# Clearing the experts' slots in sixteen pieces during batch 0 instead of eight beside the weight loads

## The chip, the cores and the metric

The kernel runs on one core of one Trainium2 chip. The metric is the device time of one execution in microseconds. Before the change it is 3038.3 us, the median of three runs (3036.37, 3038.3 and 3043.93). A fourth execution was taken with the hardware profiler on; it lasted 3023.01 us, and all rows below are from it.

## What is computed

Two layers, each cross attention and a mixture of experts, on 32 sequences of 256 tokens with 256 features:

```python
x = x + L0_xattn(layernorm(x), ctx, ctx, Wq..bo)          # 16 heads, with projections
x = x + L0_ffn(layernorm(x), P_w, U1, U2, U3, W1, W2, b2) # 12 dense experts in each of two mixtures, top 3
x = x + L1_xattn(layernorm(x), ctx, ctx)                  # 16 heads, no projections
x = x + L1_ffn(layernorm(x), router_w, w_gate, w_up, w_down, ws_gate_up, ws_down)

def L0_ffn(x, ...):
    h = gelu(sum_e C1[:, e] * (x @ W1[e].T))              # "mixture" 1
    return sum_e C2[:, e] * (h @ W2[e].T) + C3 @ b2       # "mixture" 2

def L1_ffn(x, ...):                                       # 8192 tokens, 64 experts, top 8
    pos = cumsum(onehot)[...] - 1;  valid = pos < 128     # each expert has 128 slots
    x_buf = zeros((64 * 128 + 1, 256)).at[where(valid, e * 128 + pos, 64 * 128)].set(x[tok])
    y = silu(x_buf @ w_gate) * (x_buf @ w_up) @ w_down
    return segment_sum(y[slot] * w, tok) + shared_expert(x)
```

The `zeros` of `x_buf` is what the change concerns: a slot that no token takes must hold something harmless, since each expert reads all of its 128 slots at the end.

## The kernel before

**The five queues.** The kernel is written as five programs, one for each engine (`sync_program` at L342, `gpsimd_program` at L474, and those of ScalarE, VectorE and TensorE). All of them walk the same list `order`, made by `pieces()` at L77, and each picks the steps that concern it. A step has a place, a number in units of which 40 are one batch: batch b's steps stand at 40 b plus their entry in `PLACES`, `MIX`, `HALF_PLACES` or `SCATTER`. So the tables set the order on every engine, and the engines wait for each other by semaphores only. An engine works strictly in its order.

**SyncE** (SP in the rows) issues all the plain transfers, each engine instruction going into one hardware queue. It stops where a transfer has to wait for data or for a free buffer, and everything behind it in the list stops too.

**The start.** `sync_program` first loads constants and three chunks of attention weights. Then the list starts. The 12 steps `w_mix`, at the places `W_MIX` (1, 3, 5, 11, 13, 15, 21, ... 35), load the two mixtures' weights in 12 chunks of 128x1024 floats, 512 KB each. They go through two stage buffers in turn (`x_mem` and `router_mem` in the rows); ScalarE (L573, `w_h`) and VectorE (L731, `w_l`) split each chunk in a rounded part and the rest, and a chunk's load waits until the one before the last is split (`v_w`). On VectorE and ScalarE these splits stand in the same order as the first batch's attention work.

**Clearing.** The slots lie in HBM (`expert_slots`, 64 experts x 128 slots, each row 321 floats). Right behind each of the first eight chunk loads, `sync_program` issues one transfer (L425) that writes one 321-float row, `empty_rows`, which lies in SBUF, to the 128 slots of eight experts: 128x8x321 floats, 1284 KB. Behind the eighth follow two transfers of 128 KB that clear spare rows of the output (L430). The same SBUF memory, `row_mem`, later takes batch 0's routed rows, so VectorE's write to it (L789 with `row_mem` as output) waits for `c_init`, and so does the scatter on GpSimd.

**Attention.** Each batch goes through attention twice, A in layer 0 and C in layer 1, each in two halves of eight heads. The halves are numbered u = 0, 1, 2, ... in the order of the list. For a half, SyncE reads keys and queries back from HBM (`spread`: two transfers L404 into `kst`, then two L407 into `qst`, which wait until the stores of the query parts `q_parts`, L356, have landed). Then TensorE has four score steps `s1` (L1117, into `first`), each reduced to row maxima by VectorE (L822, `nm`) before the next may overwrite the bank. The maxima are turned, brought into `qst` by four small transfers (L415, `mT`), and four `s2` steps (L1135) make the scores that ScalarE exponentiates (L653). Buffers of three halves are there, so a spread is issued when the half three before has passed its last `s2`.

**The rest of a batch** is the mixtures: 24 products (L1215) spread through the whole period, so that TensorE has work beside the attention of other batches. After the last batch the 64 experts run.

Of the kernel before, what the change touches and what calls it, by code (L numbers as in the profile page):

```python
# [15 lines left out]
P = 128  # L16
EPS = 1e-5
SENTINEL = -1.0e30
TAKEN = -3.0e30
EMPTIED = 8  # L20


class Queue:
# [48 lines left out]
}  # L72
SCATTER = tuple(158.5 + 2.5 * i for i in range(16))
W_MIX = tuple(10 * s + 1 + 2 * k for s in range(4) for k in range(3))


def pieces(NB, L, NE):  # L77


    halves = sorted((SUBS * b + HALF[kind][h], kind, b, h) for kind in "AC" for b in range(NB) for h in range(2))  # L80
    number = {u[1:]: i for i, u in enumerate(halves)}
    J = {}
    for _, kind, b, h in halves:
        J.setdefault((kind, b), len(J))
    placed = [(p, ("w_mix", i)) for i, p in enumerate(W_MIX)]
    for b in range(NB):
        for what, p in PLACES.items():
            piece = (what[:3], what[3], b) if what[:2] == "ln" else (what, b)
            placed.append((SUBS * b + p, piece))
        placed += [(SUBS * b + p, ("mix", b, n, e)) for n in range(2) for e, p in enumerate(MIX[n])]  # L90
        placed += [(SUBS * b + p, ("scatter", b, i)) for i, p in enumerate(SCATTER)]
        for kind in "AC":
            for h in range(2):
                job = (kind, b, J[kind, b], h, number[kind, b, h])
                for what, table in HALF_PLACES.items():
                    at = table[kind, h]
                    for i, p in enumerate(at):
                        placed.append((SUBS * b + HALF[kind][h] + p, (what, *job, i) if len(at) > 1 else (what, *job)))
    placed.sort(key=lambda v: v[0])
    yield from (piece for _, piece in placed)  # L100
    for e in range(NE + 2):
        if e < NE:
            yield ("e_turn", e)
        if e < NE and e % 2:
            yield ("e_same", e // 2)
        if 0 <= e - 1 < NE:
            yield ("e_gate", e - 1)
        if e >= 2:
            yield ("e_down", e - 2)


def build(nc, x_in, ctx_in, ctxT_in, wqT_in, wkvT_in, woT_in, qk_cols_in, bv_cols_in, bo_in, pw_in, uT_in,
# [28 lines left out]
    with ctx:  # L141
# [200 lines left out]
        def sync_program(sp):  # L342
# [15 lines left out]

            for c in range(FIRST):
                load_chunk(c)  # L360
            emptied = 0
            slots = slots_dram.rearrange("(e c) f -> c e f", c=CAP)
            for what, *a in order:
                if what == "load_x":
# [7 lines left out]
                elif what == "load_ctx":  # L372
                    b, = a
                    sp.wait_ge(p_c, b)
                    sp.wait_ge(p_v, min(NB, max(0, b - 3)))
                    sp.e.dma_start(ctxT[:, :, :], ctxT_in[b].rearrange("(a p) s -> p a s", p=P)).then_inc(c_ctxT, 16)
                elif what == "load_v":
                    b, = a
                    sp.wait_ge(p_c, min(NB, b + 4))
                    sp.wait_ge(p_v, b)  # L380
                    sp.e.dma_start(ctx_tok[:, :, :], ctx_in[b].rearrange("(t p) d -> p t d", p=P)).then_inc(c_ctx, 16)
                elif what == "ctx_split":
                    b, = a
                    sp.wait_ge(a_c, b + 1)
                    sp.wait_ge(p_c, b + 1)
                    store_parts(k_dram[1, b], ctx_parts, KEY_PARTS, c_kc)
                elif what == "store_K":
                    b, = a
                    sp.wait_ge(v_k, 2 * (b + 1))
                    store_parts(k_dram[0, b], k_nat, KEY_PARTS, c_k)  # L390
                elif what in ("store_A", "store_C"):
                    b, = a
                    J = job_J[what[-1], b]
                    sp.wait_ge(v_q, q_parts_of(J))
                    store_parts(q_dram[J], q_nat, QUERY_PARTS, c_q)
                elif what == "spread":
                    layer, b, J, h, u = a
                    done, ks = (c_k, k_dram[0, b]) if layer == "A" else (c_kc, k_dram[1, b])
                    sp.wait_ge(done, 48 * (b + 1))
                    if u >= 3:  # L400
                        sp.wait_ge(t_s2, 4 * (u - 2))
                    sp.wait_ge(p_const, 2)
                    for k in range(2):
                        sp.e.dma_start(row_block(k_st[u % 3], k, 0, K1), heads_of(ks, h, k)).then_inc(c_spread[u % 3], 16)  # L404
                    sp.wait_ge(c_q, 48 * (J + 1))
                    for k in range(2):
                        sp.e.dma_start(row_block(q_st[u % 3], k, 0, K1), heads_of(q_dram[J], h, k)).then_inc(  # L407
                            c_spread[u % 3], 16)
                elif what == "max_rows":
                    kind, b, J, h, u = a  # L410
                    sp.wait_ge(a_mT, u + 1)
                    for part in range(2):
                        for k in range(2):
                            r0 = (part * 2 + k) * HP
                            sp.e.dma_start(row_block(q_st[u % 3], k, K1 + part, 1),  # L415
                                           mT[u % 2][r0:r0 + HP, :].bitcast(F32)).then_inc(c_m[u % 2], 16)
                elif what == "d_down":
                    b, = a
                    sp.wait_ge(v_xd, b + 1)
                    sp.e.dma_start(out_rows(b), X[b % NXB][:, :, :]).then_inc(c_out[b % 2], 16)  # L420
                elif what == "w_mix":
                    load_chunk(FIRST + a[0])
                    if emptied < NE:
                        sp.wait_ge(p_const, 1)
                        sp.e.dma_start(slots[:, emptied:emptied + EMPTIED, :],  # L425
                                       empty_rows.unsqueeze(1).broadcast_to([P, EMPTIED, ROW])).then_inc(c_init, 16)
                        emptied += EMPTIED
                        if emptied >= NE:
                            for i in range(2):
                                sp.e.dma_start(out_pad[T + i * P:T + (i + 1) * P, :], empty_rows[:, 0:D]).then_inc(c_init, 16)  # L430
                elif what == "e_turn":
                    e, = a
                    if e == 0:
                        sp.wait_ge(t_av, 2 * HALVES)
                        sp.wait_ge(v_w, CHUNKS)

                        def load_expert(n):
                            sp.e.dma_start(ewgu[n], wgu_in[n]).then_inc(c_gu[n], 16)
                            sp.e.dma_start(down_mem[n], wd_in[n]).then_inc(c_down[n], 16)

                        for n in range(3):
                            load_expert(n)
                        sp.wait_ge(v_co, HALVES)
                        sp.wait_ge(p_xc, NB)
                        sp.wait_ge(a_out, HALVES)
                        sp.wait_ge(t_out, HALVES)
                        for s_ in c_scat:
                            sp.wait_ge(s_, 128 * NB)
                        for n in range(NX):
                            sp.e.dma_start(erow[n], slots_dram[n * CAP:(n + 1) * CAP, :]).then_inc(c_er[n], 16)  # L450
                            if n == 2:
                                for s_ in c_out:
                                    sp.wait_ge(s_, 16 * (NB // 2))
                                load_expert(3)
                                load_expert(4)
                elif what == "e_gate":
                    e = a[0] + NW
                    if e < NE:
                        sp.wait_ge(t_eg, e - NW + 1)
                        sp.e.dma_start(ewgu[e % NW], wgu_in[e]).then_inc(c_gu[e % NW], 16)  # L460
                elif what == "e_down":
                    e = a[0] + NW
                    if e < NE:
                        sp.wait_ge(t_ed, e - NW + 1)
                        sp.e.dma_start(down_mem[e % NW], wd_in[e]).then_inc(c_down[e % NW], 16)
                    e = a[0] + NX
                    if e < NE:
                        sp.wait_ge(v_ey, e - NX + 1)
                        sp.wait_ge(v_id, 2 * ((e - NX) // 2 + 1))
                        sp.e.dma_start(erow[e % NX], slots_dram[e * CAP:(e + 1) * CAP, :]).then_inc(c_er[e % NX], 16)  # L470
# [926 lines left out]
```

## Time and profile before

| | before |
|---|---|
| median of three runs | 3038.3 us |
| the profiled execution | 3023.01 us, its span 3021.2 us |
| TensorE busy | 2738.9 us, 91% |
| VectorE busy | 2202.1 us, 73% |
| ScalarE busy | 1039.7 us, 34% |
| GpSimd busy | 820.5 us, 27% |
| the hardware queue that SyncE feeds | 304.20 MB, 35.6% of 16 DMA engines' span |

TensorE is busy nine tenths of nearly every fortieth of the span; the first two fortieths (a slice is 75.5 us) and the experts at the end are the exceptions. In the span's first two slices the DMA engines are busier than in the steady part, and TensorE's granted clock is at its lower level for most of them. In the rows, PEclk is the granted clock as a share of 2.4 GHz, where 0.50 is the level of 1.2 GHz. A time in brackets at the end of a row is how long the engine stood idle before it, and who released it.

### The profile page before, as it was taken

The numbers are of one execution on the slowest core, as the hardware profiler recorded it, in microseconds if no ns is written. First come the engines' busy times: TensorE is split into PE (matmuls) and PEld (weight loads), VectorE is DVE, ScalarE is ACT, GpSimd is POOL, SyncE is SP. The second block draws the span as 40 slices with busy tenths as digits, with TensorE's granted clock in tenths as the row PEclk, the third lists the DMA queues.
The fourth block names the chain that finished last, engine by engine and source line by source line (L and its number), as shares of the span: only waits on it lengthen the run. The fifth ranks groups of instructions, "written<-read, shape, count | busy, mean of one in ns | idle before, by whom it ended". The sixth has DMA issues, their size and how long they took to land. (4 is left out here: it accounts for less than half of the span.)

```text
span 3021.2 us, 61482 instructions
## 1 busy us (share of the span) xinstructions
PE 2738.9 (91%) x23816; PEld 2297.6 (76%) x23816; DVE 2202.1 (73%) x5944; ACT 1039.7 (34%) x1524; POOL 820.5 (27%) x858
## 2 busy tenths in 40 slices
PE   2599999999999999999999999999999999956886
PEld 1388888888888888888888888888888888736775
DVE  2467888887888887888888888888888888733332
ACT  1223433333334333333333333333333333211111
POOL 1000122222222222222222222222222222334334
PEclk7599999999999999999999999999999999967998
DMA  6633444443333333333333333333333331117785
GB/s 196 183 87 97 114 124 111 116 116 110 108 96 89 100 100 100 94 86 94 100 95 94 100 89 100 98 89 83 97 99 100 99 90 43 40 39 211 207 213 126
DMA packets 321183, 327.31 MB, mean 108 GB/s; under 512 B 45405, under 2 KB 302231, under 8 KB 320892
## 3 DMA queue, kind: packets, MB, share of 16 engines
q1 hardware_dynamic: 287100, 304.20, 35.6%
q0 software_dynamic: 33792, 19.17, 3.6%
q8 instruction: 189, 3.10, 0.4%
q14 instruction: 102, 0.84, 0.1%
HBM read 182.18 MB, written 212.37 MB: 131 GB/s over the span
## 5 line engine op out<-in xcount | busy, mean ns | idle before, releaser
L653 ACT ACTIVATE exps<-second 128x1024 f32<-128x1024 f32 x512 | 525.9, 1027 | 785.0 <-PE second L1135 777.1
L548 POOL DMA_INDIRECT expert_slots<-row_mem,sidx x512 | 509.1, 994 | 790.9 <-PE first L1117 553.8
L1215 PE MATMUL mixp<-w_h,r_part_h 128*128 128x256 f32 x3072 | 668.5, 299 | 40.1 <-DVE hid L906 24.0
L822 DVE TENSOR_REDUCE nm<-first 128x4 f32<-128x1024 f32 x512 | 623.2, 1217 | 93.1 <-PE first L1117 93.0
L1215 PE MATMUL mixp<-w_h,r_part_l 128*128 128x256 f32 x3072 | 609.7, 280 | 0.0
L1215 PE MATMUL mixp<-w_l,r_part_h 128*128 128x256 f32 x3072 | 609.3, 279 | 0.0
L1215 PEld LDWEIGHTS mixp<-w_h,r_part_h 128*128 128x128 f32 x3072 | 467.4, 189 | 97.0 <-DVE hid L906 31.7
L1215 PEld LDWEIGHTS mixp<-w_l,r_part_h 128*128 128x128 f32 x3072 | 468.4, 188 | 0.0
L1215 PEld LDWEIGHTS mixp<-w_h,r_part_l 128*128 128x128 f32 x3072 | 468.1, 188 | 0.0
L906 DVE SCALAR_TENSOR_TENSOR x_mem<-mixp,C,x_mem 128x256 f32<-128x256 f32 x768 | 329.6, 477 | 114.6 <-PE mixp L1215 114.2
L906 DVE SCALAR_TENSOR_TENSOR hid<-mixp,C,hid 128x256 f32<-128x256 f32 x704 | 300.7, 474 | 35.8 <-PE mixp L1215 33.8
L1117 PE MATMUL first<-kst,qst 48*128 48x256 f32 x2048 | 248.6, 322 | 61.6 <-DVE nm L822 32.1
L517 POOL TENSOR_TENSOR norm<-norm,minus_half 128x2 f32<-128x2 f32 x128 | 92.3, 721 | 732.6 <-DVE norm L767 731.7
L1151 PE MATMUL attn_out<-exps,vx 128*17 128x256 f32 x4096 | 268.6, 390 | 3.6 <-ACT exps L653 3.4
L1135 PE MATMUL second<-qst,kst 50*128 50x256 f32 x2048 | 239.8, 313 | 16.0 <-ACT exps L653 9.3
L1117 PEld LDWEIGHTS first<-kst,qst 48*128 48x128 f32 x2048 | 159.1, 191 | 117.1 <-DVE nm L822 45.1
L1135 PEld LDWEIGHTS second<-qst,kst 50*128 50x128 f32 x2048 | 158.3, 189 | 70.2 <-issue 35.6
L1151 PEld LDWEIGHTS attn_out<-exps,vx 128*17 128x17 f32 x4096 | 98.4, 98 | 110.6 <-ACT exps L653 23.3
L561 POOL DMA_INDIRECT out<-x_mem,sidx x64 | 99.2, 1550 | 177.4 <-DVE sidx L997 127.6
L659 ACT COPY out_sb<-attn_out 128x512 f32<-128x512 f32 x128 | 74.6, 583 | 176.7 <-PE misc L1162 121.1
L588 ACT ACTIVATE nat_h<-misc,qk_cols 128x256 fp32r<-128x256 f32 x128 | 53.8, 472 | 168.8 <-PE misc L1094 168.8
L762 DVE BATCH_NORM_STATS2 norm<-x_mem 128x6 f32<-128x256 f32 x256 | 95.6, 415 | 4.1 <-POOL x_mem L531 2.8
(211 smaller groups left out, 3687.0 us busy)
## 6 DMA issues: line engine op xcount, KB each, us to landing
kst<-k_parts SPq DMA_DIRECT2D x256, 192.0 KB, 3.8
qst<-q_parts SPq DMA_DIRECT2D x256, 192.0 KB, 4.1
q_parts<-nat_h SPq DMA_DIRECT2D x128, 256.0 KB
k_parts<-ctx_part_h SPq DMA_DIRECT2D x64, 256.0 KB, 2.4
k_parts<-nat_h SPq DMA_DIRECT2D x64, 256.0 KB, 2.4
q_parts<-nat_l SPq DMA_DIRECT2D x64, 256.0 KB
exps<-in_wgu SPq DMA_DIRECT2D x39, 384.0 KB, 4.4
expert_slots<-row_mem SPq DMA_DIRECT2D x8, 1284.0 KB, 12.5
```

The costliest lines, as they stand in the source:

```text
L517: pool.e.tensor_tensor(rstd[kind][:, :], veps[kind][:, :], minus_half[:, :], ALU.pow).then_inc(p_pow[kind], 1)
L548: pool.e.indirect_dma_start(out=slots_dram, out_offset=bass.IndirectOffsetOnAxis(ap=sidx[b % 2][:, t, k:k + 1], axis=0), in_=row[b % 2][:, ...
L561: pool.e.indirect_dma_start(out=out_pad, out_offset=bass.IndirectOffsetOnAxis(ap=eid[e % NID], axis=0), in_=ey[e % NY], in_offset=None, bo ...
L653: act.e.activation(exps[:, j % NU, :, :, :].rearrange("p k t s -> p (k t s)"), second[:, :, :].rearrange("p k s -> p (k s)"), ACT.Exp, sca ...
L659: act.e.copy(out_sb[:, :, :].rearrange("p g s -> p (g s)"), attn_out[:, :]).then_inc(a_out, 1)
L762: dve.e.bn_stats(st[:, t, :], src[:, t, :]).then_inc(*seq.up())
L822: dve.e.tensor_reduce(nm[u % 2][:, :, 2 * j:2 * j + 2].rearrange("p t k -> p k t"), first[:, :, :].rearrange("p k (t s) -> p k t s", t=TIL ...
L906: dve.e.scalar_tensor_tensor(acc, src, c, acc, ALU.mult, ALU.add).then_inc(v_mix, 1)
L1117: m = pe.e.matmul(bank1[k][:, t * S:(t + 1) * S], q_st[u % 3][at, j, t * P:(t + 1) * P], k_st[u % 3][at, j, :], start=True, stop=True)
L1135: m = pe.e.matmul(bank2[k][:, s * S:(s + 1) * S], k_st[u % 3][at, j, s * P:(s + 1) * P], q_st[u % 3][at, j, :], start=True, stop=True)
L1151: m = pe.e.matmul(attn_out[r0:r0 + HD + 1, q * S:(q + 1) * S], vx[:, s, h * H // 2 + HQ * q + i, :], exps[:, (2 * q + i // 2) % NU, i % 2, ...
L1215: m = pe.e.matmul(mixp[q % 2][:, t * D:(t + 1) * D], src[i][:, dt, t * P:(t + 1) * P], wmix[n][j][:, l, dt, :], start=(k == 0), stop=(k == ...
```

## The change

`EMPTIED` becomes 4, so a clearing transfer covers four experts (128x4x321 floats, 642 KB) and there are 16. They no longer follow the chunk loads but are steps of their own, `empty`, at the places 68, 71.5, ... 120.5 of the list, which in batch 0's terms is from the end of its first mixture until after its layer-1 attention has begun. The two transfers for the output's spare rows follow the last.

```diff
-EMPTIED = 8
+EMPTIED = 4
+EMPTY = tuple(68 + 3.5 * i for i in range(16))
-    placed = [(p, ("w_mix", i)) for i, p in enumerate(W_MIX)]
+    placed = [(p, ("w_mix", i)) for i, p in enumerate(W_MIX)] + [(p, ("empty", i)) for i, p in enumerate(EMPTY)]
-            emptied = 0
                 elif what == "w_mix":
                     load_chunk(FIRST + a[0])
-                    if emptied < NE:
-                        sp.wait_ge(p_const, 1)
-                        sp.e.dma_start(slots[:, emptied:emptied + EMPTIED, :],
-                                       empty_rows.unsqueeze(1).broadcast_to([P, EMPTIED, ROW])).then_inc(c_init, 16)
-                        emptied += EMPTIED
-                        if emptied >= NE:
-                            for i in range(2):
-                                sp.e.dma_start(out_pad[T + i * P:T + (i + 1) * P, :], empty_rows[:, 0:D]).then_inc(c_init, 16)
+                elif what == "empty":
+                    n = a[0] * EMPTIED
+                    sp.wait_ge(p_const, 1)
+                    sp.e.dma_start(slots[:, n:n + EMPTIED, :],
+                                   empty_rows.unsqueeze(1).broadcast_to([P, EMPTIED, ROW])).then_inc(c_init, 16)
+                    if n + EMPTIED == NE:
+                        for i in range(2):
+                            sp.e.dma_start(out_pad[T + i * P:T + (i + 1) * P, :], empty_rows[:, 0:D]).then_inc(c_init, 16)
```

The waits on `c_init` are written with `NE // EMPTIED + 2` and so rise from 10 transfers to 18. The instructions of TensorE, VectorE, ScalarE and GpSimd stand in the same order as before; only SyncE's list moves. One line is added ahead of the programs, so most line numbers rise by one.

The first place is SyncE's list at the start, from the spread of half 0 on. Before, a clearing transfer stands behind each chunk (`in_w1T`):

```order
L376 DMA ctxT<-in_ctxT 128x2x256
L352 DMA x_mem<-in_w1T 128x1024 [waits dve_w]
L425 DMA expert_slots<-row_mem 128x8x321
L352 DMA router_mem<-in_w1T 128x1024 [waits dve_w]
L425 DMA expert_slots<-row_mem 128x8x321
L404 DMA kst1<-k_parts 48x4x256 x2
L407 DMA qst1<-q_parts 48x4x256 x2
L370 DMA x_mem<-in_x 128x2x256
```

And now:

```order
L376 DMA ctxT<-in_ctxT 128x2x256
L353 DMA x_mem<-in_w1T 128x1024 [waits dve_w]
L353 DMA router_mem<-in_w1T 128x1024 [waits dve_w]
L404 DMA kst1<-k_parts 48x4x256 x2
L407 DMA qst1<-q_parts 48x4x256 x2
L370 DMA x_mem<-in_x 128x2x256
```

The clearing transfers between the chunks and ahead of the spread of half 1 are gone.

The second place is SyncE's list at the end of the clearing, around the row maxima of half 6 (`qst0<-mT`) and the spread of half 8 (`kst2`, `qst2`). Before:

```order
L415 DMA qst0<-mT 1x4x256 x3
L381 DMA ctxT<-in_ctx 128x2x256
L356 DMA q_parts<-nat_h 128x2x256 [waits dve_q]
L356 DMA q_parts<-nat_l 128x2x256
L356 DMA q_parts<-nat_h 128x2x256
L404 DMA kst2<-k_parts 48x4x256 [waits pe_s2,k_parts_out]
L404 DMA kst2<-k_parts 48x4x256
L407 DMA qst2<-q_parts 48x4x256 [waits q_parts_out]
L407 DMA qst2<-q_parts 48x4x256
```

And now:

```order
L415 DMA qst0<-mT 1x4x256 x3
L381 DMA ctxT<-in_ctx 128x2x256
L426 DMA expert_slots<-row_mem 128x4x321
L357 DMA q_parts<-nat_h 128x2x256 [waits dve_q]
L357 DMA q_parts<-nat_l 128x2x256
L357 DMA q_parts<-nat_h 128x2x256
L426 DMA expert_slots<-row_mem 128x4x321 x3
L430 DMA out<-row_mem 128x256 x2
L404 DMA kst2<-k_parts 48x4x256 [waits pe_s2,k_parts_out]
L404 DMA kst2<-k_parts 48x4x256
L407 DMA qst2<-q_parts 48x4x256 [waits q_parts_out]
L407 DMA qst2<-q_parts 48x4x256
```

One piece now stands ahead of the stores of the query parts, and three with both spare-row transfers stand between those and the spread that TensorE needs next. Of the other twelve pieces, two stand ahead of the query parts for half 4 and two ahead of its spread, three around the spread of half 5, two ahead of the query parts for half 6 and one behind its spread, one behind the key parts before the maxima of half 5, and one between those maxima and the spread of half 7.

## Rows read from the trace of the kernel before

**Rows 1.** The page: TensorE's granted clock in 40 slices of the span

```profile
PEclk7599999999999999999999999999999999967998
```

**Rows 2.** Busy time by stretch: PE, PEld, DVE, ACT, POOL, clock, DMA share, GB/s

```profile
30.00:60.00 30.00, 3.06 (x16) 2.01 (x16) 8.14 (x8) 3.60 (x5) 0.00 (x0) 0.56 0.99 272
...
120.00:146.00 26.00, 15.97 (x70) 12.98 (x70) 15.68 (x45) 3.63 (x5) 0.69 (x1) 0.55 0.35 75
...
180.00:300.00 120.00, 114.37 (x1012) 98.54 (x1013) 93.34 (x234) 37.06 (x53) 7.90 (x9) 0.96 0.34 91
```

**Rows 3.** Timeline, first 90 us, TensorE and ScalarE: start us, duration us, engine, line

```profile
46.32 0.80 PE L1117 MATMUL first<-kst,qst 48*128 48x256 f32 x4 [16.73 <-DMA qst<-q_parts]
...
53.71 1.04 ACT L573 CAST w_h<-router_mem 128x1024 fp32r<-128x1024 f32 x1 [4.78 <-DMA router_mem<-in_w1T]
...
57.20 0.80 PE L1117 MATMUL first<-kst,qst 48*128 48x256 f32 x4 [7.98 <-DVE nm L822]
...
60.16 1.23 DVE L822 TENSOR_REDUCE nm<-first 128x4 f32<-128x1024 f32 x1 [0.89 <-PE first L1117]
...
62.38 0.80 PE L1117 MATMUL first<-kst,qst 48*128 48x256 f32 x4 [2.26 <-DMA qst<-q_parts]
...
79.75 1.02 ACT L653 ACTIVATE exps<-second 128x1024 f32<-128x1024 f32 x1
...
84.15 1.04 ACT L573 CAST w_h<-x_mem 128x1024 fp32r<-128x1024 f32 x1 [3.39 <-DMA x_mem<-in_w1T]
...
87.64 0.80 PE L1117 MATMUL first<-kst,qst 48*128 48x256 f32 x4 [12.58 <-DVE nm L822]
```

**Rows 4.** SyncE's queue in the same stretch, start and duration of issues

```profile
36.43 2.07 SPq L407 DMA_DIRECT2D qst<-q_parts  x2
...
40.15 3.07 SPq L352 DMA_DIRECT2D router_mem<-in_w1T  x1
...
75.34 0.67 SPq L352 DMA_DIRECT2D x_mem<-in_w1T  x1
```

**Rows 5.** Transfers by line over the span: KB each, median us from issue to landing

```profile
qst<-q_parts SPq DMA_DIRECT2D x256, 192.0 KB, 4.1
...
expert_slots<-row_mem SPq DMA_DIRECT2D x8, 1284.0 KB, 12.5
...
x_mem<-in_w1T SPq DMA_DIRECT2D x3, 512.0 KB, 8.8
router_mem<-in_w2T SPq DMA_DIRECT2D x3, 512.0 KB, 4.2
x_mem<-in_w2T SPq DMA_DIRECT2D x3, 512.0 KB, 4.9
```

**Rows 6.** SyncE's queue in batch 0's mixtures: spreads of halves 4, 6, 7 and 8

```profile
176.77 0.79 SPq L407 DMA_DIRECT2D qst<-q_parts  x2
...
224.54 0.79 SPq L407 DMA_DIRECT2D qst<-q_parts  x2
...
241.14 0.93 SPq L407 DMA_DIRECT2D qst<-q_parts  x2
...
250.27 0.44 SPq L381 DMA_DIRECT2D ctxT<-in_ctx  x1
...
256.20 0.79 SPq L407 DMA_DIRECT2D qst<-q_parts  x2
```

**Rows 7.** TensorE at the first s1 of halves 4, 6, 7 and 8

```profile
192.92 0.51 PE L1117 MATMUL first<-kst,qst 48*128 48x256 f32 x4
...
233.56 0.40 PE L1117 MATMUL first<-kst,qst 48*128 48x256 f32 x4
...
247.42 0.40 PE L1117 MATMUL first<-kst,qst 48*128 48x256 f32 x4
...
263.91 0.40 PE L1117 MATMUL first<-kst,qst 48*128 48x256 f32 x4
```

**Rows 8.** VectorE's first write over the cleared row's memory, which waits for the clearing

```profile
303.90 0.73 DVE L789 TENSOR_SCALAR row_mem<-x_mem,norm 128x256 f32<-128x256 f32 x2
```

## The prediction

> **What bounds the kernel now.** I read the page first, for TensorE's clock by slices, then busy times by stretch, then the timeline of the first 90 us on TensorE and ScalarE, and last SyncE's queue and the transfers' times to landing, at the start and again where the clearing goes. In the steady part TensorE is the bound: from 180 to 300 us it is busy 114.4 of 120 us while the DMA engines are busy 34% of the time [rows 2]. At the start it is the reverse. From 30 to 60 us TensorE is busy 3.06 of 30 us, the DMA engines 99%, at 272 GB/s [rows 2]. Those 30 us move some 8.2 MB, and four clearing transfers of 1284 KB, 5.3 MB, are issued in them, so about two thirds of the traffic is clearing that nothing needs before VectorE's write at 303.90 [rows 8]. The reader is to see in [rows 3] that the start is a chain of waits for transfers: the first score product at 46.32 waited 16.73 us for its queries, the split of a weight chunk at 53.71 waited for its load, the score product at 57.20 waited for VectorE, which had that chunk's other half to make first, the one at 62.38 waited for queries again, and the split at 84.15 waited for a load. So there are two questions: how much of the start comes back, and what 16 pieces cost in the steady part, where TensorE has no time to spare.
>
> **The price of a piece.** A chunk of 512 KB into `x_mem` lands in 4.9 us where no clearing is about (`in_w2T`) and in 8.8 us at the median where one stands just ahead of it (`in_w1T`) [rows 5]. The difference, 3.9 us for 1284 KB, is 329 KB/us, and a piece of 642 KB is 1.95 us of the queue.
>
> **What is removed at the start.** First, the chunk that SyncE issues at 40.15 [rows 4] is split from 53.71 on [rows 3], 13.6 us later. Without clearing it lands in 4.2 to 4.9 us [rows 5], at 44.4 to 45.1. SyncE is there no later than now, since the load waits only for the chunk split before it. I take 9.0 us off; the score product at 57.20 follows this split on VectorE by a fixed 3.5 us and goes with it. The wait ahead of the product at 46.32 is then off the path: its queries, last issued before 38.5 [rows 4], land by 42.6 with the median 4.1 us [rows 5], and the product behind it still waits for that chunk on VectorE. Second, the product at 62.38 waited for queries; the reduction that frees its bank ended at 60.16 + 1.23 = 61.39 [rows 3], so 0.9 us more. Third, the chunk issued at 75.34 [rows 4] would land at 80.2 instead of 84.15, but ScalarE is in an exponential until 79.75 + 1.02 = 80.8 [rows 3]: 3.4 us more, and the product at 87.64 follows. Together 9.0 + 0.9 + 3.4 = 13.3 us off. Behind 90 us the chunk loads already land in 4.2 and 4.9 us, and what is late there is the chain of ScalarE, VectorE and TensorE itself, at 1.2 GHz.
>
> The ends for this term: if the first chunk lands in 8.8 us as those behind a clearing do, because the spreads crowd it just as well, its part is 13.6 - 8.8 = 4.8 us and the rest small, so 5 us. At the other end, from 120 to 146 us TensorE is busy 16.0 of 26 us at a mean clock of 0.55 [rows 2]; a denser start may lift the clock earlier, and if half of that work ran at 2.4 GHz it would save 4 us, for 17. I take 13.3, as each of its three pieces has a row.
>
> **What is added in the steady part.** The eight more issues cost SyncE about 0.45 us each (its other issues are of that length), which it has. No engine waits for the pieces but at 303.90 [rows 8], and the last is issued at about 256, 40 us before. So the price is in what is queued behind them, and on each spread I compare the landing of its queries with TensorE's first use. All times here are those of before; the whole pattern moves forward together.
>
> Half 6: two pieces stand ahead of its query parts. The second of its query loads leaves at about 225.0 and lands 4.1 us later, at 229.1; two pieces make it 233.0, and TensorE comes at 233.56 [rows 6, 7]. Cost nothing, with 0.6 us to spare. Half 4 has four pieces ahead, 7.8 us, on a landing at 181.3 and a use at 192.92 [rows 6, 7]: nothing, and half 5's spread is issued right behind for the four products that follow. Half 7: one piece stands ahead of the spread. Second load at 241.6, landing at 245.7; with 1.95 and 0.45 for the issue 248.1, against 247.42 [rows 6, 7]: 0.7 us late. Half 8: one piece ahead of the query parts, three and the two spare-row transfers behind them. From 250.27 [rows 6] the queue takes 256 KB of context, the piece, 768 KB of query parts, three pieces, 256 KB of spare rows and 768 KB of spread, 4616 KB in all; at 329 KB/us that ends at 264.3. The median landing of 4.1 us [rows 5] has 2.3 us of its own spread's 768 KB in it, so 1.8 us remain for the way there and back: 266.1, against TensorE's 263.91 [rows 7]. That is 2.2 us late. The 0.7 of half 7 is contained in it, since SyncE reaches this stretch through the maxima of half 6, which TensorE turns before it gets to half 7. The maxima themselves (L415) stand behind pieces that were issued some 4 us before; I put them at nothing. The ends: nothing at all, if the pieces run faster than 329 KB/us; and, if half 8's queries, issued at 256.20 and landing by 260.8, come later by all four pieces and the spare rows (8.6 us), 269.4, or 5.5 us. I take 2.2, from the count of bytes.
>
> **The sum.** 13.3 off and 2.2 on is 11.1 us off. Against the profiled execution of 3023.0 us (its span is 3021.2) that is 3011.9. The median of the three runs stands 15.3 us above the profiled execution, which I take as the level of the runs and not as part of the change: 3038.3 - 11.1 = 3027.2 us, or 0.37% faster. What a measurement of this kernel can tell from no change is about 0.3%, 9.1 us.
>
> **The rivals.** (1) The start gives back less. The chunk loads are two buffers deep and their splits are interleaved with the score reductions, so a chunk that lands early meets a ScalarE or VectorE that is not free. For it: 8.14 of VectorE's first 30 us are work in a fixed order [rows 2]. Against: both engines' wait rows name the transfer. With 8 off and 2 on, 3032. (2) The clock rises earlier and stays: 4 us more off, 3023. For it the denser start, against it the page, where the second slice is at 0.5 [rows 1] although TensorE is busy over half of the time from 120 to 146. (3) Each piece pays a fixed time in the queue of its own. A 512 KB load lands in 4.2 us [rows 5], of which its bytes at 329 KB/us are 1.6; if the other 2.6 held the queue too, the four pieces ahead of half 8's spread would add 10.4 us, and the sum would be 13.3 off and 12.6 on: 3037.6. Against: four transfers of a spread, 768 KB, land 4.1 us after the last issue, so fixed times overlap.
>
> The Trainium skill, "DMA: Bandwidth & Descriptors", sections "Bandwidth" and "Rules for kernel authors", speaks against the change in this way: it advises at least 1 MiB per DMA and gives a fixed cost of about 2 us each. By that rule eight more transfers would be an estimated 16 us more of the queue if nothing overlapped, and the sum would come out 5 us slower where all of it met TensorE; rival 3 is what it would do at the place where it matters.
>
> (4) Slower. The pieces stand ahead of what TensorE needs next in every half, not only in half 8: the maxima and spreads all land late, and each piece is lost in full. That is 16 x 1.95 = 31.2 on and 13.3 off, 17.9 slower, 3056. It begins to lose where seven of the sixteen pieces are on the path (7 x 1.95 = 13.7). For it: margins of 0.6 us at half 6 and below nothing at 7 and 8. Against: pieces ahead of a wait of SyncE's are through before what they delay is issued, and a late half absorbs the lateness of the one behind it. That the change does not do what it says is excluded by SyncE's list, where no clearing stands before half 3's maxima.
>
> **How the numbers follow.** The forecast, between 9.1 and 14 us off, has 0.50. Rival 2 has 0.12, rival 1 0.20, rival 3 0.09, rival 4 0.09. So faster by over 0.3% is 0.50 + 0.12 = 0.62, within 0.3% is 0.20 + 0.09 = 0.29, slower 0.09. The range runs from 3020, where the start gives 17 and the pieces cost nothing (3021.3), to 3038, where rival 3 is; it leaves out rival 4 and some of the tails.
>
> **What would show it.** In the new profile: the first score product near 41 instead of 46.32, the one at 57.20 near 48, the one at 87.64 near 74; DMA share from 30 to 60 well under 0.99. Then, between 165 and 260, DMA share up from 0.34, with TensorE waiting for `qst<-q_parts` once or twice, 1 to 3 us in all. The prediction is wrong if waits for `qst` or `kst` add up to over 6 us there, if maxima (`qst<-mT`) show as releasers, or if the product at 87.64 moves by under 9 us.

## The result and the profile after

The changed kernel takes 3027.58 us, the median of twelve runs (3020.72 to 3035.74), against 3036.38 us for the kernel before in the same comparison (twelve runs, 3033.5 to 3046.68). The recorded ratio is 0.9966, 95% interval 0.9953 to 0.9978: some 10 us faster, 0.34%. (A recorded ratio is not the quotient of the two medians, which is 0.9971 here; in this study the two differ by up to 0.0008.) It was compared twice more in the course of the experiments and gave 0.9967 (0.9955 to 0.9979) and 0.9971 (0.9959 to 0.9983).

The profiled execution lasted 3025.41 us, 2.4 us more than the profiled one of before. A single execution does not show this gain at its end. Landmarks show why: the gelu near 400 us and the one near 2602 us are 2203.1 us apart in the profile of before, and 2206.1 to 2218.8 us in the 13 others of this study, whose lists are the same in that stretch on all engines; the changed kernel's own three have 2207.0, 2209.6 and 2210.3. So I read each trace up to the gelu near 400 us and leave the time to the repeated runs.

The page of the changed kernel, TensorE's clock in 40 slices, and busy times by stretch with the columns of [rows 2] (the line numbers of SyncE's instructions are one higher than before, those of the other engines' rows shown here are unchanged):

```profile
PEclk9699999999999999999999999999999999957998
...
30.00:60.00 30.00, 6.84 (x32) 5.14 (x32) 10.69 (x11) 5.46 (x7) 0.00 (x0) 1.00 0.69 166
...
120.00:146.00 26.00, 20.54 (x138) 18.09 (x139) 18.45 (x52) 4.28 (x7) 1.97 (x2) 0.74 0.09 32
146.00:180.00 34.00, 30.38 (x269) 24.68 (x268) 16.27 (x43) 14.36 (x20) 0.69 (x1) 0.95 0.73 204
180.00:300.00 120.00, 113.02 (x955) 96.40 (x954) 93.62 (x241) 34.74 (x50) 9.28 (x11) 0.93 0.50 143
```

From 30 to 60 us the DMA share falls from 0.99 to 0.69 and TensorE's busy time doubles; from 180 to 300 us the share rises from 0.34 to 0.50, and TensorE loses a little. The clock of 0.74 from 120 to 146 us, 0.55 before, is no faster start: the steady part, which follows half 2's copy, has moved into that stretch. The 26 us that correspond to it, 12.4 us earlier, look as before:

```profile
107.60:133.60 26.00, 15.97 (x70) 12.98 (x70) 15.59 (x45) 3.66 (x5) 0.69 (x1) 0.54 0.36 76
```

The timeline of the start, to be held against [rows 3]:

```profile
42.88 0.80 PE L1117 MATMUL first<-kst,qst 48*128 48x256 f32 x4 [12.96 <-DMA qst<-q_parts]
...
46.92 1.04 ACT L573 CAST w_h<-router_mem 128x1024 fp32r<-128x1024 f32 x1 [1.25 <-DMA router_mem<-in_w1T]
...
50.41 0.80 PE L1117 MATMUL first<-kst,qst 48*128 48x256 f32 x4 [4.62 <-DVE nm L822]
...
54.65 0.80 PE L1117 MATMUL first<-kst,qst 48*128 48x256 f32 x4 [1.33 <-DVE nm L822]
...
73.04 1.03 ACT L573 CAST w_h<-x_mem 128x1024 fp32r<-128x1024 f32 x1
...
76.52 0.80 PE L1117 MATMUL first<-kst,qst 48*128 48x256 f32 x4 [9.27 <-DVE nm L822]
```

The product at 57.20 is at 50.41, 6.8 us earlier; that at 62.38 at 54.65, 7.7 earlier, its wait for queries gone; that at 87.64 at 76.52, 11.1 earlier. The split at 73.04 waits for no transfer any more.

And TensorE in batch 0's mixtures, against [rows 7], where `attn_out` is the product behind the one that waits:

```profile
235.83 0.57 PE L1117 MATMUL first<-kst,qst 48*128 48x256 f32 x4 [0.76 <-DMA qst<-q_parts]
...
238.79 3.61 PE L1151 MATMUL attn_out<-exps,vx 128*17 128x256 f32 x32
...
256.49 0.72 PE L1117 MATMUL first<-kst,qst 48*128 48x256 f32 x4 [2.59 <-DMA qst<-q_parts]
257.14 3.31 PE L1151 MATMUL attn_out<-exps,vx 128*17 128x256 f32 x32
```

Two waits for queries, at halves 7 and 8. Behind each, 32 products take 3.61 and 3.31 us. In the kernel before they take 2.01; the first of its rows here is a score product between half 7's first one and those 32, which waits 1.68 us for ScalarE:

```profile
250.16 0.50 PE L1135 MATMUL second<-qst,kst 50*128 50x256 f32 x4 [1.68 <-ACT exps L653]
...
250.83 2.01 PE L1151 MATMUL attn_out<-exps,vx 128*17 128x256 f32 x32
...
264.24 2.01 PE L1151 MATMUL attn_out<-exps,vx 128*17 128x256 f32 x32
```

**The two measures used below** are ScalarE's copies of turned maxima (L647). Of half 2, at the end of the start: 146.44 us before, 134.06 after. And the distance from half 6's copy to half 7's, which holds both waits and the low clock between and behind them:

```profile
146.44 0.36 ACT L647 CAST mT<-misc 16x256 fp32r<-16x256 f32 x1 [0.47 <-PE misc L1125]
...
247.41 0.36 ACT L647 CAST mT<-misc 16x256 fp32r<-16x256 f32 x1
266.93 0.36 ACT L647 CAST mT<-misc 16x256 fp32r<-16x256 f32 x1
```

```profile
134.06 0.36 ACT L647 CAST mT<-misc 16x256 fp32r<-16x256 f32 x1 [0.38 <-PE misc L1125]
...
234.89 0.36 ACT L647 CAST mT<-misc 16x256 fp32r<-16x256 f32 x1
261.14 0.36 ACT L647 CAST mT<-misc 16x256 fp32r<-16x256 f32 x1
```

The first fence is before, the second after: 12.4 us won at the start, and a distance of 26.25 instead of 19.52 us, 6.7 us lost. ScalarE's gelu (L667) at 399.16 us before is at 393.46, 5.7 ahead, which is the difference.

### The profile page after: what moved, and what is told of

It is laid out like the page before. It is cut to its first block and busy times, and to the rows that moved or that the text cites. A ratio compares the mean times of both kernels' runs of the same rounds, so it can differ in the third digit from the quotient of the medians.

```text
span 3023.6 us, 61490 instructions
## 1 busy us (share of the span) xinstructions
PE 2752.8 (91%) x23816; PEld 2301.2 (76%) x23816; DVE 2205.9 (73%) x5944; ACT 1040.3 (34%) x1524; POOL 819.7 (27%) x858
```

## The experiments

Two questions: is the gain all from the start and the loss all from the pieces ahead of halves 7 and 8, and what sets the size of each? All fourteen profiled executions, of eleven kernels, in one table (after, after_again and after_third are one kernel, five_behind and five_again another); "gelu" is the one at 399.16 us before.

| kernel | copy of half 2 | distance 6 to 7 | gelu | ratio (95%) |
|---|---|---|---|---|
| before | 146.44 | 19.52 | 399.16 | 1 |
| after | 134.06 | 26.25 | 393.46 | 0.9966 (0.9953 to 0.9978) |
| after_again | 134.62 | 26.23 | 396.36 | 0.9967 (0.9955 to 0.9979) |
| after_third | 133.36 | 25.61 | 394.95 | 0.9971 (0.9959 to 0.9983) |
| gaps | 132.51 | 19.51 | 387.31 | 0.9955 (0.9937 to 0.9972) |
| five_behind | 133.58 | 19.52 | 386.20 | 0.9948 (0.9929 to 0.9967) |
| five_again | 133.01 | 19.54 | 386.59 | 0.9956 (0.9939 to 0.9974) |
| both | 148.73 | 25.66 | 407.63 | 1.0014 (1.0001 to 1.0027) |
| one_behind | 134.51 | 25.96 | 394.61 | 0.9983 (0.9966 to 0.9999) |
| four_behind | 133.62 | 22.19 | 391.30 | 0.9952 (0.9937 to 0.9968) |
| first4_late | 138.10 | 19.52 | 393.01 | 0.9969 (0.9956 to 0.9982) |
| last4_late | 145.02 | 19.53 | 400.07 | 0.9982 (0.9969 to 0.9996) |
| small_early | 149.48 | 19.51 | 403.05 | 0.9999 (0.9981 to 1.0018) |
| big_late | 133.95 | 24.37 | 391.44 | 0.9959 (0.9946 to 0.9972) |

**gaps: all pieces where SyncE's queue is empty.**

```diff
-EMPTY = tuple(68 + 3.5 * i for i in range(16))
+EMPTY = tuple(47.1 + 0.01 * i for i in range(8)) + tuple(87.1 + 0.01 * i for i in range(8))
```

> All sixteen pieces stand in stretches in which SyncE's queue is empty: eight behind the load of x for batch 2, eight and the two spare-row transfers behind the load of x for batch 3, each just behind a spread and over 20 us ahead of the next transfer that TensorE needs. Theory A (start gives about 12.5 us, the pieces in the steady part take back 6.7 us, 3.35 by two waits for queries at halves 7 and 8 and as much by TensorE running at 1.2 GHz behind them): no wait for qst at halves 7 and 8, the gelu at 393.46 us in the changed kernel's trace comes at 386.7 plus or minus 1, about 12.4 ahead of before's 399.16, and the time is 12 us under the kernel before, ratio 0.996. Rival B (the lateness comes from the bytes as such, wherever they stand): the gelu stays at 393 and the ratio at 0.9966 to 0.998.

Measured: distance 19.51, gelu at 387.31, ratio 0.9955. The same bytes cost nothing that this distance shows where nothing that TensorE needs is queued close behind them; rival B falls.

**five_behind: the last five pieces go behind the spreads.**

```diff
-EMPTY = tuple(68 + 3.5 * i for i in range(16))
+EMPTY = tuple(68 + 3.5 * i for i in range(11)) + (108.43,) + tuple(121.1 + 0.01 * i for i in range(4))
```

> Only the last five of the sixteen pieces move, by one place each in SyncE's list: the one ahead of the spread of half 7 goes behind it, the four around the query parts and ahead of the spread of half 8 go behind that spread. Theory A: both waits for queries (0.76 and 2.59 us in the changed kernel's trace) and the half-speed stretches behind them go, the gelu near 393.5 comes at 386.7 to 387.5, the time is about 6 us under the changed kernel. Rival C (the two waits cost only themselves, 3.35 us, and the low clock there came by chance): gelu at 390. Rival B: no change, 393.

Measured: gelu at 386.20, ratio 0.9948, no wait for queries, both `attn_out` rows at 2.01 us:

```profile
237.90 2.01 PE L1151 MATMUL attn_out<-exps,vx 128*17 128x256 f32 x32
...
251.31 2.01 PE L1151 MATMUL attn_out<-exps,vx 128*17 128x256 f32 x32
```

The whole 6.7 us comes back, not only the 3.35 us of the two waits, so theory A holds for the sum. Its split of the sum, half waiting and half low clock, does not hold, as four_behind shows below. The eleven pieces that stayed cost nothing that this stretch shows.

**both: the price of the late pieces alone.** The slots are cleared early as before, and the late pieces go to a spare tensor.

```diff
                     load_chunk(FIRST + a[0])
+                    if a[0] < 8:
+                        sp.e.dma_start(slots[:, 8 * a[0]:8 * a[0] + 8, :],
+                                       empty_rows.unsqueeze(1).broadcast_to([P, 8, ROW])).then_inc(c_init, 16)
...
-                    sp.e.dma_start(slots[:, n:n + EMPTIED, :],
+                    sp.e.dma_start(spare[:, n:n + EMPTIED, :],
```

> The slots are cleared early, in eight transfers beside the chunk loads as before, and the sixteen late pieces are issued as well, to a spare tensor of the same shape. So the start is that of before and only the price of the late pieces is left. By the prediction's term this is 2.2 us slower than before, gelu at 401.4. Theory A says 6.7 us, gelu at 405.9, ratio about 1.002.

Measured: ratio 1.0014, 0.3 to 8.2 us slower, which holds both 2.2 and 6.7. The trace is sharper: distance 25.66, 6.1 us over before's, with waits of 0.88 and 2.05 us. The gelu came even later than expected, 407.63, because this execution's start was 2.3 us behind before's (148.73).

**after_again: the changed kernel unchanged.**

> The changed kernel once more, unchanged, beside the others. Gelu at 393.5 plus or minus 0.5 if the stretch up to there repeats from run to run; ratio 0.9966 as before; if the clock behind the two waits falls by chance, the gelu moves by 1 to 3 us between executions.

Measured: ratio 0.9967. The gelu came 2.9 us later than expected, at 396.36, so the stretch up to it does not repeat to half a microsecond; most of the difference stands between the maxima of halves 3 and 4. There TensorE's clock, at its lower level in every execution for some us, came back later, as the same stretch in after and then in after_again shows:

```profile
206.00:208.00 2.00, 2.00 (x19) 2.00 (x19) 2.00 (x3) 0.00 (x0) 0.00 (x0) 1.00 1.11 384
...
206.00:208.00 2.00, 2.00 (x11) 1.67 (x11) 1.80 (x6) 0.25 (x1) 0.47 (x1) 0.50 0.02 6
```

The copies of halves 3 and 4 are 48.1 to 48.2 us apart in five of the fourteen executions (after_again, gaps, four_behind, first4_late, last4_late) and 46.3 to 46.4 in the other nine, whatever the kernel, and the clock comes back later in just those five. So the gelu column holds some 2 us that are not the edit's. The distance 6 to 7 did repeat, 26.23.

**first4_late and last4_late: which early transfers matter.** Eight transfers of 1284 KB; four stay behind their chunks, four go to the empty stretch.

```diff
-EMPTIED = 4
-EMPTY = tuple(68 + 3.5 * i for i in range(16))
+EMPTIED = 8
+EMPTY = (13.01, 15.01, 21.01, 23.01, 87.1, 87.11, 87.12, 87.13)     # first4_late
+EMPTY = (1.01, 3.01, 5.01, 11.01, 87.1, 87.11, 87.12, 87.13)        # last4_late
```

> Clearing in eight transfers of 1284 KB. The first four, which before are issued between 33 and 54 us, go to the empty stretch behind the load of x for batch 3; the other four stay behind their chunk loads at 74 to 96 us. By the prediction's terms the score products of the first 60 us move by 9.0 + 0.9 us and the chunk at 75.34 still lands late, so the copy of the maxima of half 2 (L647), at 146.44 us before, comes at 136.5 us. Rival (chunks that land early meet busy engines): 141 or later. No wait for queries in the steady part, so the time is 10 us under before, ratio 0.9967.

> The mirror of the last: the four clearing transfers between 33 and 54 us stay, the four between 74 and 96 us go to the empty stretch. By the prediction's third term the maxima of half 2 (L647) come 3.4 us earlier, at 143.0 instead of 146.44. If clearing at 74 to 96 us costs more than the one chunk, 141. Ratio 0.998 to 0.999.

Measured: 138.10 and 145.02 us, 8.3 and 1.4 us ahead of before, each less than expected, the first between the forecast and the rival's 141 and nearer to the forecast. For the second, half 0's copy shows why: that execution had been 2.0 us behind before's already (71.73 against 69.71). Counted from that row, half 2 comes 73.3 us later and not 76.7 (77.0 in both, 77.5 in small_early), 3.4 us less, the expected size. The rows of last4_late:

```profile
71.73 0.36 ACT L647 CAST mT<-misc 16x256 fp32r<-16x256 f32 x1 [2.11 <-PE misc L1125]
...
145.02 0.36 ACT L647 CAST mT<-misc 16x256 fp32r<-16x256 f32 x1 [0.38 <-PE misc L1125]
```

Both ratios, 0.9969 and 0.9982, are gains by themselves, in the order expected.

**one_behind and four_behind: is the loss at half 8 on top of that at half 7?** Only the twelfth piece moves behind its spread, or only the last four.

```diff
-EMPTY = tuple(68 + 3.5 * i for i in range(16))
+EMPTY = tuple(68 + 3.5 * i for i in range(11)) + (108.43,) + tuple(110 + 3.5 * i for i in range(4))   # one_behind
+EMPTY = tuple(68 + 3.5 * i for i in range(12)) + tuple(121.1 + 0.01 * i for i in range(4))            # four_behind
```

> Of the changed kernel's sixteen pieces only the twelfth moves, from ahead of the spread of half 7 to behind it. Theory D (the landing of half 8's queries sets the loss, what is lost at half 7 is contained in it): no wait at half 7 and no half-speed stretch behind it, but the wait at half 8 grows from 2.6 to 4.5 to 5 us, and the copy of the maxima of half 7 (L647) follows that of half 6 by 26.2 us as in the changed kernel. Theory E (the two losses add): it follows by 23.5 us or less, where 19.5 is the distance in the kernel before.

> The last four pieces and the spare rows go behind the spread of half 8, the twelfth stays ahead of the spread of half 7. So only the wait of 0.8 us at half 7 is left. If the fall of TensorE's clock behind it is its doing, the maxima of half 7 follow those of half 6 by 19.5 + 0.8 + 1.5 to 2.5, 22 to 23 us; if the clock fell there for another reason, by 20.3 us.

Measured, one_behind first and four_behind second:

```profile
239.85 2.82 PE L1151 MATMUL attn_out<-exps,vx 128*17 128x256 f32 x32
...
257.73 0.61 PE L1117 MATMUL first<-kst,qst 48*128 48x256 f32 x4 [3.11 <-DMA qst<-q_parts]
258.27 3.43 PE L1151 MATMUL attn_out<-exps,vx 128*17 128x256 f32 x32
```

```profile
237.93 0.50 PE L1117 MATMUL first<-kst,qst 48*128 48x256 f32 x4 [0.84 <-DMA qst<-q_parts]
...
240.80 3.61 PE L1151 MATMUL attn_out<-exps,vx 128*17 128x256 f32 x32
...
256.41 2.01 PE L1151 MATMUL attn_out<-exps,vx 128*17 128x256 f32 x32
```

Taking the wait at half 7 away saves next to nothing, distance 25.96: theory D holds, the landing of half 8's queries sets the loss. Counted from half 6's copy, TensorE was ready for them after 16.7 to 19.3 us in the five executions with the last four pieces in place, and they came after 20.6 to 21.7 us in all five. Its size within did not come as written, a wait of 3.1 and not 4.5 to 5 us, since TensorE ran part of the way at 1.2 GHz (granted clock 0.50 from 241 to 244 us) though it had not waited for queries.

Four_behind leaves the 0.8 us wait alone and costs 22.19 - 19.52 = 2.7 us, as expected in size. But it is not 0.8 of waiting and 1.9 of low clock. The score product that follows waited 1.68 us for ScalarE in the kernel before; here it waits only 0.60:

```profile
239.65 0.80 PE L1135 MATMUL second<-qst,kst 50*128 50x256 f32 x4 [0.60 <-ACT exps L653]
```

It starts 2.74 us behind half 6's copy, and 2.75 us behind it in the kernel before, where there is no wait for queries. So the wait itself costs nothing, and the 2.7 us come behind it, where the granted clock is 0.50 from 239 to 245 us. Its ratio of 0.9952 is as good as five_behind's; the runs can't separate 2.7 us.

**small_early and big_late: the size of the pieces.** Small_early puts two pieces behind each of the first eight chunk loads; big_late has `EMPTIED = 8` and eight places, `69.75 + 7 * i`.

> Sixteen pieces of 642 KB, two behind each of the first eight chunk loads: the size of the change at the place of before. If pieces cost by their bytes (329 KB/us), the copy of the maxima of half 2 (L647) comes at 146.4 plus or minus 1.5 us and the ratio is 1. If each piece holds the queue for 2.6 us of its own (the prediction's rival 3), eight more transfers make the stretch 10 to 20 us longer: 156 or later, ratio 1.003 to 1.006.

> Eight transfers of 1284 KB at the place of the change, one for each pair of pieces: the place of the change with the size of before. By bytes, half 7's queries now stand behind a whole 1284 KB and are 2 us later than in the changed kernel, a wait of 2.5 to 3 us, and half 8's land as late as there, so that the maxima of half 7 follow those of half 6 by 26 us again, ratio 0.9967 to 0.998. If small pieces are what makes the late landing of half 8, by a fixed cost for each, the distance falls to 21 or 22 us.

Measured: small_early is at 149.48 us and 0.9999. That is outside the 1.5 us that I had allowed, but both, with eight transfers at the same place, is at 148.73, and it is far from the 156 of a fixed cost for each. So rival 3 falls. Big_late waits 3.32 us at half 7, over the 2.5 to 3 expected, and 1.01 us at half 8:

```profile
238.30 0.80 PE L1117 MATMUL first<-kst,qst 48*128 48x256 f32 x4 [3.32 <-DMA qst<-q_parts]
...
256.15 0.51 PE L1117 MATMUL first<-kst,qst 48*128 48x256 f32 x4 [1.01 <-DMA qst<-q_parts]
256.58 1.92 PE L1151 MATMUL attn_out<-exps,vx 128*17 128x256 f32 x32
```

Half 8's queries land at 256.15 us where after's landed at 256.49, 21.3 us behind half 6's copy where after's came 21.6 behind it, so by bytes it is the same. The distance is 24.37 and not 26, because here TensorE's 32 products behind the wait took 1.92 us: the clock did not fall. Neither place shows a difference between pieces of 642 KB and of 1284 KB.

**five_again and after_third: the best version beside the changed kernel.**

> The version with the last five pieces behind the spreads, again, beside the changed kernel on the same chip. If its 6.7 us up to the maxima of half 7 (L647) last to the end: 6 to 8 us under the changed kernel, ratio 0.9945 to 0.995; the maxima of half 7 follow those of half 6 by 19.5 us. If what was gained there is lost again later in the steady part, where executions differ by some us anyway, the two ratios are alike.

> The changed kernel beside it: ratio 0.9966 again, maxima of half 7 behind those of half 6 by 26.2 us in every execution, of which 3.2 to 3.4 us are the two waits for queries.

Measured: 0.9956 and 0.9971. After_third waited 4.7 us in all and not 3.2 to 3.4, at halves 7 and 8:

```profile
236.28 0.50 PE L1117 MATMUL first<-kst,qst 48*128 48x256 f32 x4 [0.76 <-DMA qst<-q_parts]
...
238.76 2.01 PE L1151 MATMUL attn_out<-exps,vx 128*17 128x256 f32 x32
...
255.94 0.80 PE L1117 MATMUL first<-kst,qst 48*128 48x256 f32 x4 [3.91 <-DMA qst<-q_parts]
```

The clock held behind the first wait, TensorE came to half 8 earlier, and waited there for what it had gained: 255.94 against 256.49. Five_behind and five_again are the fastest of all, 0.9948 and 0.9956; the intervals of both overlap with the changed kernel's. Compared directly with it, on the same chip each time, the medians are 7.2 and 3.7 us lower (3018.08 against 3025.26, and 3025.79 against 3029.45) and the means 6.1 and 2.6 us. Resampling the recorded times gives 95% intervals of 3.2 to 8.9 us for the first pair and of -2.4 to 8.2 us for the second: a gain in the first, and not clear in the second.

## Why the prediction was right

The forecast was 3027.2 us, 11.1 us under before; the time is 3027.58 us and the gain some 10 us. The mechanism was right in its outline: a start bound by transfers gives back most, and the queries of halves 7 and 8 take a part of it. Of its two terms the start was put somewhat too small, and the price of the pieces at a third of what it is. That the time agrees to 0.4 us is in part luck: the two errors partly cancel, and the level that the forecast started from, 3038.3 us, was 1.9 us above the median of the twelve runs.

**The start, 13.3 us.** In the two profiles it is 12.4 us at half 2's copy. The three steps: the chunk issued at 40.15 before was worth 6.8 us and not 9.0; the freed wait for queries 0.9, as forecast (5.18 us from one product to the next before, 4.24 after); the chunk issued at 75.34 was worth 3.4, as forecast. The three landmarks came at 42.88, 50.41 and 76.52 us where I had written near 41, 48 and 74. The step that failed is "SyncE is there no later than now" and the landing in 4.2 to 4.9 us: SyncE issued the load at 40.96, since the chunk split before it was itself 1.2 us later, and it landed in 5.9 us. The row of its issue in the changed kernel:

```profile
40.96 0.34 SPq L353 DMA_DIRECT2D router_mem<-in_w1T  x1
```

A spread is issued right behind this load, which may be what slowed it, as I had supposed for the lower end of the term; no run separates that. In return 1.3 us came between 88 and 146 us, where I had put nothing. The profile of before was at the fast end: half 0's copy is at 69.71 us in it and at 71.73 to 72.03 in the three others with the same clearing ahead of it (last4_late, both, small_early). The three executions with all clearing early have half 2's copy at 146.44, 148.73 and 149.48 us, mean 148.2, and the nine with none of it early at 132.51 to 134.62, mean 133.7. So the start is worth about 14.5 us, between 12 and 17 by the extremes of the two groups.

**The pieces, 2.2 us.** Half 6 no wait, as forecast. Half 7 late by 0.7 us, measured 0.76 to 0.88 in the five executions with that piece; the wait is taken up by the one for ScalarE behind it. That half 7's loss is contained in half 8's was shown by one_behind. What failed is half 8's landing, 2.2 us late by the count of bytes at 329 KB/us. Moved forward by the 12.5 us of half 6's copy it should have come at 253.6, and it came at 256.49, 2.9 us later: 5.1 us late, near the upper end of 5.5 that I had given for this term. The stretch in question, in the changed kernel:

```profile
237.70:240.00 2.30, 2.30 (x20) 1.35 (x24) 1.79 (x2) 1.39 (x2) 0.00 (x0) 0.50 0.33 87
...
250.00:255.00 5.00, 3.90 (x34) 3.56 (x32) 4.00 (x7) 2.64 (x3) 0.00 (x0) 1.00 1.07 222
250.00:256.50 6.50, 3.91 (x36) 3.60 (x34) 4.00 (x7) 2.64 (x3) 0.00 (x0) 1.00 0.84 175
```

Between the first two of these the DMA engines moved 379 and then 304 GB/s at full share. But the first 2.3 us moved 87 GB/s, and the 5 us that hold the spread 222, at full share too; in the 1.5 us before the product starts nearly nothing moves. So one rate for everything, from the first issue on, was too fast; what makes spreads slower I did not test.

The trace of before would have shown it. The count gives 266.1 - 8.6 = 257.5 for the same queries without pieces, and there they were issued at 256.20 and landed by about 260.1:

```profile
L407 SPq DMA_DIRECT2D qst<-q_parts x2: 303/374/444, 256.2 to 256.5; - x2
...
DMA to landing us min/median/max: 3.3/3.5/3.6
```

That is 12.7 us behind half 6's copy, and 21.6 us behind it in the changed kernel: four pieces and the spare rows made it 8.9 us later, and their bytes at 329 KB/us are 8.6. The price of a piece was right; the landing that it was added to was not.

The second thing missing is the clock. I had looked for it at the start only (rival 2), and it mattered here: behind the wait at half 8 the 32 products took 3.31 to 3.61 us instead of 2.01 in five of five executions with a wait over 2 us there. The pieces cost 6.1 to 6.7 us in the four executions of the full pattern (the changed kernel's three, and both). Of these 4.1 to 5.2 us are the late landing, counted from the 16.5 us behind half 6's copy at which TensorE came to half 8 before, and 1.5 to 2.0 us the low clock behind it. One_behind has 4.8 and 1.6, and big_late, where the clock did not fall there, 4.8 and nothing. 14.5 off and 6.5 on make 8 us, which lies in the intervals of all three comparisons of the changed kernel.

**The rivals.** Rival 1 (less from the start) was true of the size of its first step only, and not by its mechanism: the split at 46.92 waited 1.25 us for its load, no engine was busy with something else. (The 8.14 us that I named for it are VectorE's between 30 and 60 us, not in its first 30.) Rival 2 did not come: from 30 to 60 us the granted clock is 1.00 instead of 0.56, yet the products of that stretch still take 0.80 us for four, as before, and in the 26 us up to half 2's copy, which it named, the clock is 0.54 as against 0.55. Rival 3 is refuted by small_early: twice as many transfers of half the size made a ratio of 0.9999 (0.9981 to 1.0018), at most 5.5 us slower, where the forecast's estimate for a fixed cost that never overlaps was 16 us. The Trainium skill, "DMA: Bandwidth & Descriptors", section "Rules for kernel authors", advises at least 1 MiB per DMA; these runs show no difference between 642 and 1284 KB, which is no test of smaller ones. The fixed cost of about 2 us that the forecast took from that page stands in its section "Anatomy of one DMA — SWDGE (gpsimd) path", for transfers that GpSimd issues, and not in the two that the forecast names. Rival 4, every piece lost in full for 31.2 us, did not come: the eleven pieces that five_behind left in place cost nothing visible, and the other five together 6.1 to 6.7 us. But the mechanism it names, pieces ahead of what TensorE needs next, is the one that made the loss three times my 2.2 us. Of the signs of being wrong that I had set, none came: in the changed kernel the waits for queries add up to 3.35 us and not over 6, no copied maxima show as what TensorE waited for between 165 and 260 us, and the product at 87.64 moved by 11.1 us.

## What to carry to other kernels

Work that nobody waits for should leave a stretch that is bound by transfers, but where it goes decides half of the gain: directly behind the transfers that the busy engine needs next or into a stretch where the queue is empty, not directly ahead of them. Here it was the bytes queued ahead of a needed transfer that counted, and no difference between pieces of 642 and of 1284 KB showed. A count of bytes should first be run on the kernel before, where the trace has the answer. A wait of TensorE can cost more than its length, since the products behind it may run at the lower clock: four_behind's wait cost nothing itself and the low clock behind it 2.7 us.

## What was not expected of the hardware

TensorE's clock did not answer a wait in the same way each time. With 0.76 to 0.88 us of waiting at half 7, the 32 products behind took 3.61 us in four executions (after, after_again, both, four_behind) and 2.01 us in one (after_third). Without a wait for queries they took 2.01 us in seven of eight executions and 2.82 us in one_behind. In big_late, with 3.32 us of waiting, they took 2.69. TensorE stands idle there without it too, 1.68 us for ScalarE in the kernel before, so whether the wait for queries is what made the clock fall in the four is likely from these counts but not shown. The granted clock in the stretch from 237.70 to 240 us of the changed kernel, shown above, is 0.50, which is the lower level of 1.2 GHz. The Trainium skill, "TensorE: Matmul & The Clock Gate", section "What's actually happening", says that recent activity sets the clock, full or half; the two lengths, the longer 1.8 times the shorter, fit two levels, and these executions show that the same program can fall on either side.

Identical steady work differed by up to 16 us over 2200 us between profiled executions (2203.1 to 2218.8 us between the two gelus), more than the effect under study. Landmarks near the change repeated far better: the distance between two copies was 19.51 to 19.54 us in all seven executions in which no queries of halves 7 and 8 landed late. Even so near a landmark the clock can shift things: the distance between the copies of halves 3 and 4 took two values, 1.8 us apart.
